# Two-layer RGAT kernel: W1's first relation loaded in front of x, ten of its k tiles done in front of the pair loop, codes stored by ScalarE, last maxima transposed at once

## What is computed

```python
xr = jnp.einsum('nd,rdf->rnf', x, W)          # R=3 relations, F=768
oi, oj = xr[etype, dst], xr[etype, src]
alpha = leaky_relu(oi @ q + oj @ k, 0.2)      # per edge and head
m = segment_max(alpha, dst)
e = exp(alpha - m[dst]); z = segment_sum(e, dst)
msg = e / (z[dst] + 1e-16) * oj               # per head
out = segment_sum(msg, dst) + b
# h = elu(rgat(x, W1, ...)); y = layernorm(x + rgat(h, W2, ...))
```

## Time and profile before

| what | value |
|---|---|
| median of three runs | 1361.34 us (1356.54 to 1362.07) |
| profiled execution | 1356.26 us |
| its span | 1354.5 us |
| TensorE busy | 1283.6 us (95%) |
| VectorE busy | 1072.3 us (79%) |
| ScalarE busy | 769.3 us (57%) |
| granted TensorE clock, mean | 0.976 of 2.4 GHz |

### The profile page before, as it was taken

One profiled execution on the slowest core, in us unless ns is written; L12 is line 12 of the kernel. 1 busy time (PEld: TensorE's weight loads), 2 busy tenths in 40 slices (PEclk: granted clock), 3 DMA queues, 4 the chain that ended last, 5 costly groups with the idle time before them and its releaser, 6 DMA issues.

```text
span 1354.5 us, 19301 instructions
## 1 busy us (share of the span) xinstructions
PE 1283.6 (95%) x7042; PEld 1158.6 (86%) x7042; DVE 1072.3 (79%) x1447; ACT 769.3 (57%) x1291; POOL 6.5 (0%) x21
## 2 busy tenths in 40 slices
PE   5789999999979999999999999999979999999994
PEld 4787665666659999999999999999979999999994
DVE  3667889999849989989989976868837667867874
ACT  3354453232249979989989964237525445554562
POOL 1000000000000000000000000000000000000000
PEclk9688999999989999999999999999999999999998
DMA  8212013111153333333333225864467766677561
GB/s 288 106 71 83 30 42 122 47 47 47 41 186 109 98 98 98 101 96 98 100 96 94 61 75 175 282 235 159 158 210 289 270 219 200 210 248 237 187 203 45
DMA packets 84952, 188.38 MB, mean 139 GB/s; under 512 B 8189, under 2 KB 59198, under 8 KB 84866
## 3 DMA queue, kind: packets, MB, share of 16 engines
q1 hardware_dynamic: 84674, 186.65, 41.7%
q0 software_dynamic: 192, 0.57, 0.1%
HBM read 147.59 MB, written 39.61 MB: 138 GB/s over the span
## 4 chain that ended last, share of the span: by engine, by line
PE 77%; DVE 13%; ACT 4%; DMA 3%; issue 2%; SPq 0%; DVEq 0%; ACTq 0%
PE ps L1110 23%; PE ps L1055 23%; PE ps L921 14%; PE ps L944 9%; PE ps L965 4%; DVE arena L1235 2%; PE ps L903 2%; DVE arena L1291 2%; DVE arena L1295 1%; ACT arena L703 1%; DMA arena<-in_L_gnn_W 1%; DMA Ct<-in_x 1%; ACT arena L704 1%; DVE ps L1363 1%; DVE arena L1376 1%
## 5 line engine op out<-in xcount | busy, mean ns | idle before, releaser
L1055 PE MATMUL ps<-arena 128*128 128x193 f32 x2400 | 398.3, 328 | 1.8 <-DVE arena L1295 1.5
L1055 PEld LDWEIGHTS ps<-arena 128*128 128x128 f32 x2400 | 393.8, 190 | 4.2 <-DVE arena L1295 3.6
L921 PE MATMUL ps<-arena,xT 128*128 128x384 f32 (+1 forms) x720 | 245.2, 490 | 0.0
L703 ACT ACTIVATE arena<-arena,misc 128x640 f32<-128x640 f32 x240 | 197.1, 821 | 32.8 <-DVE arena L1291 23.4
L921 PEld LDWEIGHTS ps<-arena,xT 128*128 128x128 f32 x720 | 132.4, 191 | 80.4 <-issue 4.6
L704 ACT ACTIVATE arena<-arena,misc 128x640 f32<-128x640 f32 x240 | 195.9, 816 | 0.0
L1291 DVE TENSOR_TENSOR arena<-arena 128x1280 f32<-128x1280 f32 x120 | 178.4, 1487 | 20.3 <-ACT arena L704 18.1
L1295 DVE SCALAR_TENSOR_TENSOR arena<-arena,Ct 128x1280 f32<-128x1280 f32 x120 | 179.2, 1493 | 14.0 <-DVE arena L1291 9.6
L1110 PE MATMUL ps<-g_hi,x2a 128*128 128x416 f32 (+1 forms) x540 | 154.3, 355 | 9.9 <-DVE g_lo L1450 8.5
L1235 DVE SCALAR_TENSOR_TENSOR arena<-arena,misc 128x1250 f32<-128x1250 bf16 x108 | 155.8, 1517 | 2.2 <-ACT arena L642 2.2
L1110 PE MATMUL ps<-g_hi,x2b 128*128 128x416 f32 (+1 forms) x540 | 152.2, 351 | 0.0
(11 more groups left out here) (172 smaller groups left out, 1501.4 us busy)
## 6 DMA issues: line engine op xcount, KB each, us to landing
x2a<-xr_d SPq DMA_DIRECT2D x41, 768.0 KB, 4.5
x2b<-xr_d SPq DMA_DIRECT2D x41, 768.0 KB, 4.4
arena<-xr_d SPq DMA_DIRECT2D x120, 193.0 KB, 2.4
xr_d<-stg SPq DMA_DIRECT2D x60, 384.0 KB, 3.1
arena<-ab_d SPq DMA_DIRECT2D x12, 1280.0 KB, 6.4
arena<-in_L_gnn_W SPq DMA_DIRECT2D x6, 2304.0 KB, 9.2
xr_d<-bb SPq DMA_DIRECT2D x60, 193.0 KB, 2.4
arena<-in_L_gnn_W SPq DMA_DIRECT2D x7, 1152.0 KB, 6.7
```

The costliest lines, as they stand in the source:

```text
L703: nc.scalar.activation(e1[t % 5][:, h, :], abr[:, r, h, :], ACT.Exp, bias=qk1t[:, t, col + R * H:col + R * H + 1])
L921: last = mm(unit1_bank(u)[:, 0:w], xT[:, kt, t * P:(t + 1) * P], v, start=kt == 0, stop=kt == KT - 1)
L1055: last = mm(bank1(g, i)[:, o:o + HD + 1], e1[t % 5][:, h, i * P:(i + 1) * P], xring[t % NX][:, o:o + HD + 1], start=False, stop=True, skip ...
```

## The change

- SyncE loads W1's relation 0 in three pieces of two k tiles, each with a semaphore of its own (`w_first`), in front of x. `load_w(0)` is gone. The two code stores go to ScalarE's list, as its first instructions.
- TensorE does W tiles 0 to 5 and products 0 to 3 first, the rank matmul in front of W tile 2 (now into bank 1). Then it waits for `row_ready` and transposes x. The run transposes stand in front of the second group of x, where they were in front of the third. W tiles 6 to 9 and products 4 to 7 follow. ScalarE's stores go the same way.
- PRE is 10; the eight W tiles left stand at every third pair (0, 3, ... 21), products at pairs 0, 1, 2, 5, ... 23, and T_AT becomes 25.
- All ten tiles of the last relation's maxima are transposed in front of unit 54, and the ab rows in front of unit 55.
- ScalarE's first exponential step stands in front of the store of unit 59.

```diff
@@ constants
-        PRE = 4
-        WT_AT = {(i - PRE) * 7 // 3: i for i in range(PRE, R * KT)}
+        PRE = 10
+        WT_AT = {3 * (i - PRE): i for i in range(PRE, R * KT)}
...
-                {54: (0, 4), 55: (4, 7), 56: (7, 10)}]
+                {54: (0, 10)}]
...
-        AB1_AT = 57
+        AB1_AT = 55
...
-            return w_in[n % 2], 16 * (n // 2 + 1)
+            return w_in[n % 2], 16 * (n // 2 + n % 2)
@@ sync
-            sp.wait_ge(S["code_ready"], 1)
-            sp.dma_start(code_d[0:E].rearrange("(p c) -> p c", p=EP), code[0:EP, :]).then_inc(S["code_out"], 16)
-            sp.dma_start(code_d[E:E + PADL].rearrange("(a c) -> a c", a=1), f1[0:1, 0:PADL]).then_inc(S["code_out"], 16)
+            w = W1[0].rearrange("(k p) f -> p k f", p=P)
+            for i in range(R):
+                sp.dma_start(wslot[0][:, 2 * i:2 * i + 2, :], w[:, 2 * i:2 * i + 2, :]).then_inc(w_first[i], 16)
             sp.wait_ge(S["x_zero"], 1)
...
-            load_w(0)
             load_w(1)
@@ scalar
+            act.wait_ge(S["code_ready"], 1)
+            act.dma_start(code_d[0:E].rearrange("(p c) -> p c", p=EP), code[0:EP, :]).then_inc(S["code_out"], 16)
+            act.dma_start(code_d[E:E + PADL].rearrange("(a c) -> a c", a=1), f1[0:1, 0:PADL]).then_inc(S["code_out"], 16)
...
-            for i in range(PRE):
+            for i in range(KT):
                 wt_out(i)
                 if i >= 2:
                     wq_out(i - 2)
+            n = 0
+            for t0 in range(0, NT, XG):
...
+            for i in range(KT, PRE):
+                wt_out(i)
+                wq_out(i - 2)
...
             for _, kind, i in sorted(events):
+                if kind == 0 and i == U1 - 1:
+                    act.wait_ge(ab_in[0], 16)
+                    exp_step(0, 0, 0)
                 if kind == 0 and i == AB1_AT:
                     ab_rows(L1)
@@ tensor
                 r, kt = i // KT, i % KT
-                if kt == 0:
+                if r == 0:
+                    pe.wait_ge(w_first[kt // 2], 16)
+                elif kt == 0:
                     pe.wait_ge(*landed(r))
                 if i >= 2:
                     pe.wait_ge(S["wt_ready"], i - 1)
-                if i == 1:
+                if i == KT + 1:
                     pe.wait_ge(S["edi_ready"], 1)
...
-                    pe.wait_ge(S["row_ready"], 1)
                     pe.wait_ge(S["qv_in"], 32)
...
-            for i in range(PRE):
+            for i in range(KT):
+                if i == 2:
+                    pe.wait_ge(S["ranks"], 1)
+                    for s in range(2):
+                        last = mm(ps[1][0:SW, s:s + 1], G[0:EP, s * SW:(s + 1) * SW], onesf[0:EP, 0:1], start=True, stop=True)
+                    last.then_inc(S["ranks"], 1)
                 wt_transposes(i)
                 if i >= 2:
                     wq_product(i - 2)
+            pe.wait_ge(S["row_ready"], 1)
+
+            n = 0
+            for t0 in range(0, NT, XG):
+                if t0 == 0:
+                    pe.wait_ge(S["x_in"], 16)
+                if t0 == XG:
+
+                    pe.wait_ge(S["runs_in"], 32)
...
+            for i in range(KT, PRE):
+                wt_transposes(i)
+                wq_product(i - 2)
```

More of the change, by code:

```diff
@@ L290, in rgat @@
         w_in = [sem(f"w_in{i}") for i in range(2)]
+        w_first = [sem(f"w_first{i}") for i in range(R)]
         xr_out = [sem(f"xr_out{i}") for i in range(NS1)]
@@ L672, in _, with exp_step @@
             events = [((u - NT + 1) * UNIT_T, 0, u) for u in range(NT, U1)] + [(max(0, i - MASK_LAG) * TILE_T, 1, i) for i in range(RS)]
+            def exp_step(g, r, t):
+                step = g * RS + r * NT + t
+                hp = group1(g)[0]
+                act.wait_ge(S["a_used"], step + 1)
+                act.wait_ge(S["e2_free"], step + 1)
+                for h in range(2):
+                    col = r * H + hp * 2 + h
+                    nc.scalar.activation(e1[t % 5][:, h, :], abr[:, r, h, :], ACT.Exp, bias=qk1t[:, t, col + R * H:col + R * H + 1])
+                    last = nc.scalar.activation(e2[t % 2][:, h, :], abr[:, r, 2 + h, :], ACT.Exp, bias=ks1[:, t, col:col + 1])
+                last.then_inc(S["e_ready"], 1)
             for _, kind, i in sorted(events):
+                if kind == 0 and i == U1 - 1:
+                    act.wait_ge(ab_in[0], 16)
+                    exp_step(0, 0, 0)
                 if kind == 0 and i == AB1_AT:
```

61 lines of the change are left out of this document (21 added, 40 removed).

## The result

The changed kernel takes 1352.18 us (median of 8 runs, 1347.06 to 1355.5) against 1358.68 us (8 runs, 1356.54 to 1362.07) on the same chip: a ratio of 0.994, 95% interval 0.9926 to 0.9954. That is 8.2 us less by the ratio, 6.5 by the medians; 7.3 were forecast. The sum holds, but none of its four terms came out as written: in the profiled execution the three of the prologue and the loop gave 2.9 us where 8.3 were forecast, and the end, which was to cost 1.0, gave 2.8.

A forecast was written before the change was run, and what follows sets the result against it. The pair loop's end, set by TensorE's pair matmuls and W1 products, was taken to move everything behind it; +6.7 - 23.7 + 8.7 + 1.0 = -7.3 from 1361.34 gave 1354.0 us, range 1350 to 1358.

The forecast's parts named there:

- Term 1: Prologue: the first pair is multiplied at 48.3 us, 6.7 later, bounds 4.2 and 11.2, with the run codes landing at 28.5.
- TensorE has room up to there: Prologue: TensorE finishes W tiles, products, ranks and six x groups by about 25 us, then waits for codes landing at 28.5.
- a sign of being wrong: The forecast called itself wrong if the first pair came under 45 or over 53 us.
- Term 2: Pair loop, pairs with W tiles: 73.2 us become 49.5, bounds 42.7 and 66.8; change -23.7.
- I keep 38%: Pairs with W tiles: the share of time at 1.2 GHz stays 38%, turning 42.7 us at full clock into 49.5.
- each slow stretch before ended within 16 us: Said of the kernel before, as evidence against half clock lasting from the wait for the codes on.
- the third rival: The wait for codes at 25 us drops TensorE to half clock through the tile stage: +16.2, 1377.5 us; chance 0.08.
- the clock stays up: Rival: the tile stage runs at 2.4 GHz throughout, 42.7 us; with early codes -16.6 in all, 1344.7 us; chance 0.22.
- Term 3: Pair loop, pairs with unit steps: 68.3 us become 77.0, bounds 74 and 79, VectorE pacing one-step pairs; change +8.7.
- Term 4: From the last maximum to the first attention step: 1.0 us longer, bounds -0.6 and +1.8.
- they wait for a_used, which TensorE raises behind unit 59: End: the first exponentials wait for that count, start about 396.4 us instead of 395.35, first attention step at 402.6.
- The lower bound of -0.6: End, from last maximum to first attention step: 0.6 us shorter if TensorE raises the count ahead of its last matmuls.

The follow-up runs named there:

- ranks_first: The changed kernel with the rank matmul in front of all W tiles; 1348.84 us, 0.9927 of the kernel before.
- warm_loop: The changed kernel plus 6 zero matmuls between flag and first pair and 3 before pair-loop products from pair 2; 1343.3 us, 0.9887 of the kernel before.
- warm_both: warm_loop plus the rank matmul first and 12 zero matmuls ahead of the W tiles; 1340.93 us, 0.9851 of the kernel before.
- warm_tiles: warm_both with run transposes behind the second x group and 2 zero matmuls before each prologue product; 0.9853 of the kernel before, a 1662.66 us run left aside.
- gap_only: The changed kernel plus 6 zero matmuls in the gap ahead of the first pair, none in the loop; 1344.43 us, 0.9885 of the kernel before.

## Why the prediction came out as it did

**Term 1, forecast +6.7, measured +9.3 (within its bounds).** Two steps failed, in two places that lay side by side. The codes: they landed at 30.9, not 28.5. The price of the store beside W1 was right (3.5 us forecast, 3.7 measured in ranks_first: 6.6 against 2.9), but 1.1 us were taken off it for the ranks, though of two things that run side by side the later one counts, and the old arrival was taken to have up to 2 us to spare, where it had 0.2 (26.7 against 26.93). The gathers started 3.95 us later (13.33 against 9.38), since the rank matmul came at 11.4 and not at 10, behind W tiles at half clock; from there to the codes it took 17.6 us against 17.3 before. TensorE: I took the W tiles of the prologue at 2.1 us each, the price of the earlier trace rows, because nothing in the rows showed the clock there; at 1.2 GHz they cost 3.7, and that alone brings the run transposes to 31.8. So the step "TensorE has room up to there" was wrong in the changed kernel's profile, by 0.9 us, and right in the four others of the same prologue, in which TensorE waited 0.5 to 2.6 us for codes used at 31.4 to 32.3. Behind the codes the forecast held here: 16.6 + 2.5 us to the first pair against 17.3 + 2.5. That is in part luck: in the four others the 16.6 are 14.9 to 20.5, and two of their first pairs (53.7, 54.5) are over the 53 that the forecast gave as a sign of being wrong.

**Term 2, forecast 49.5 us, measured 55.6.** The cycle was right: where the profile shows the full clock throughout (warm_loop, warm_both, warm_tiles) the stage takes 43.4 to 43.6 us, and 42.7 was the working. The share of the slow clock was taken over from the kernel before (38%) and was 56% (17.1 us at 0.50, and 38.5 at 0.82, of which 36% is 13.9). By the forecast's own formula that gives 42.7 / (0.44 + 0.56 x 0.64) = 53.5. The failed step is "I keep 38%". The slow stretch that the earlier trace rows show from 41.6 on began at 37.1 (0.50 to 57.6, 20.5 us), while TensorE waited 3.37 us for the flag; now it begins in the W tiles ahead of the flag (44.5) and lasts 23.9 us, 17 of them in the stage, and the short ones behind it add up to as much as before (13.9 us against 12.7) in a shorter stage. So "each slow stretch before ended within 16 us", said against the third rival, was a misreading too. The rival *the clock stays up* was wrong for the changed kernel and is what warm_loop made of it. The Trainium skill's rule (TensorE: Matmul & The Clock Gate, What's actually happening), that activity releases the throttle, I had set aside because TensorE was busy 15.70 of 15.70 us at half clock. With the runs, both can stand: the busy time of a row counts an 8-column product as busy like any other, and with zero matmuls 512 columns wide in TensorE's idle time the clock came up. What in them does it was not measured.

**Term 3, forecast 77.0, measured 73.9 (just under its bound of 74).** The mis-sized term is the pair. One-step pairs were priced at VectorE's 1.34; they run at 1.31, and as before the stage takes 1.6 less than the count of its pairs says (69.9 against 68.3 before, 75.5 against 73.9 now). I had that difference in hand and didn't carry it over.

**Term 4, forecast +1.0, measured -2.7 to -2.8; outside its bounds of -0.6 to +1.8.** The transposes, reductions, ab rows and units came as worked out (9.9 us to the ab transposes against 10.05, units through 30.5 behind the last maximum against 30.8). The failed step is "they wait for a_used, which TensorE raises behind unit 59". TensorE's list had raised the count while that unit was still being multiplied, at most 0.6 us behind its first matmul (389.09); exp began at +27.1 and not +30.8. The lower bound of -0.6 named this very case, but gave it 1.6 us where it was worth 3.8. The second half of that step, the store of unit 59 at the end of its matmuls, was wrong as well: it waits for its staging buffer, whose write stands behind the ab loads in SyncE's list. That queue I had not followed.

**Sum.** Terms 1 to 3 were 2.6, 6.1 and -3.1 off, 5.6 too good together by the profile (2.7 by the runs), and term 4 was 3.8 too bad (3.7 by the runs). The total was right by luck: two errors of opposite sign took each other away.

## What to carry to other kernels

Read TensorE's speed from the durations of a form that occurs at both clocks, not from its busy share: rows of small transposes and products 8 columns wide were busy all the time here at 1.2 GHz (17.70 of 17.70 us). A few wide matmuls of zeros in time that is idle anyway were worth about as much as the whole reordering: 7.5 us for six of them (gap_only against the changed kernel, by the ratios), 12 for all of warm_both, against 8.2. No run has the zeros in the kernel before, so whether they would do without the reordering stays open. When an edit moves loads ahead in one engine's in-order list, follow what stood behind them; a buffer's write there held up a store on another engine. When two paths meet at one wait, shortening one alone shows nothing.

## What the hardware showed that was not expected

- Up to the first recorded change the granted clock read 1.00 whatever the durations said: 17.7 us of W tiles at 2.57 us a product stood under 1.00.
- TensorE's semaphore increment behind unit 59 was visible to ScalarE 3.4 us before that unit's last matmul ended (389.68 against 393.1), and by as much in every kernel with the early exponentials. An increment that stands by itself in TensorE's list is no sign that the matmuls ahead of it are done.
- A DRAM store of 156 KB took 2.9 us from issue to use on idle DMA engines and 6.6 us beside a 2.3 MB load on another queue (ranks_first). The Trainium skill (Trainium Kernel Development and Optimization, Key Constraints) has it that the queues share the same 16 engines and interleave; the trace agrees: the store, issued at 6.4, was used at 13.0, ahead of the last third of the load, which was issued at 4.3 and landed at 13.5.
- The same lists led to first pairs 5 us apart in five profiles, by when the clock fell and rose in the W tiles; from the last pair to the last maximum all fourteen agree within 0.1 us.
